# The returned rows of an expert stage: scaled on ScalarE, added on VectorE in groups of eight tiles

## What is computed

```python
x = x + 0.5 * L0_ffn(layernorm(x))      # stage 0, "f": experts
x = x + L0_attn(layernorm(x))           # stage 1, "s": scan
x = x + 0.5 * L0_ffn(layernorm(x))      # stage 2, "f": experts
x = x + 0.5 * L1_ffn(layernorm(x))      # stage 3, "m": soft mixture
x = x + L1_attn(layernorm(x))           # stage 4, "a": attention
x = x + 0.5 * L1_ffn(layernorm(x))      # stage 5, "m": soft mixture

# L0_ffn, for a token row x: one expert of eight, weighted by its probability
gate_probs = softmax(x @ gate_w.T)
e = argmax(gate_probs)
out = (relu(x @ w1[e] + b1[e]) @ w2[e] + b2[e]) * gate_probs[e]
```

## Time and profile before

| | us |
|---|---|
| median of 3 runs | 1003.56 |
| lowest and highest | 1002.2 and 1004.35 |
| the profiled execution | 1003.07 |
| span of its trace | 1001.3 |
| VectorE at L694, 64 instructions | 19.5 |
| VectorE idle until the returned rows land, twice | 14.2 |

### The profile page before, as it was taken

The page is one execution under the profiler, slowest core; times in us unless marked ns, Lnnn a source line. Parts: engine busy times, 40 slices in busy tenths (PEclk is TensorE's granted clock), DMA queues, the critical chain, the costliest instruction groups (busy, mean ns, idle before and its releaser), DMA issues.

```text
span 1001.3 us, 18706 instructions
## 1 busy us (share of the span) xinstructions
PE 777.1 (78%) x5564; PEld 512.1 (51%) x5564; DVE 658.6 (66%) x2367; ACT 507.3 (51%) x1371; POOL 442.9 (44%) x563
## 2 busy tenths in 40 slices
PE   4788983798498960499666979988999899729977
PEld 3678872547288860377651323333333333327757
DVE  4565654775865548856387776877777886566634
ACT  5333331606133323866411466767767677687650
POOL 1047773400277762411156577486585633261100
PEclk9999997895599995699895678999989999959999
DMA  6731113002011113000021342242231200000002
GB/s 154 230 92 49 50 47 99 1 1 84 13 46 52 50 37 82 0 1 1 1 45 32 59 58 37 31 63 34 38 54 31 48 4 3 1 1 1 1 1 84
DMA packets 53426, 42.95 MB, mean 43 GB/s; under 512 B 9861, under 2 KB 48722, under 8 KB 53328
## 3 DMA queue, kind: packets, MB, share of 16 engines
q1 hardware_dynamic: 46784, 31.74, 15.4%
q0 software_dynamic: 4992, 9.32, 3.4%
q10 hardware_dynamic: 1552, 0.70, 0.3%
HBM read 18.27 MB, written 11.40 MB: 30 GB/s over the span
## 4 chain that ended last, share of the span: by engine, by line
PE 42%; DVE 18%; POOL 12%; issue 12%; ACT 9%; DMA 5%; ACTq 1%; DVEq 1%; POOLq 0%; SPq 0%
PE psum L1498 5%; POOL arena L832 4%; DMA result_rows<-arena,scatter_row 3%; PE psum L1269 3%; PE psum L747 3%; DVE half_stats L444 3%; PE psum L1483 2%; DVE cst L1565 2%; PE psum L1232 2%; PE psum L1241 2%; PE psum L1438 2%; PE psum L787 2%; DVE x L694 2%; PE psum L1332 2%; PE psum L799 2%
## 5 line engine op out<-in xcount | busy, mean ns | idle before, releaser
L1565 DVE CUSTOM_DVE_ANT_0 cst<-psum,rot 128x512 bf16<-128x512 f32 (+3 forms) x512 | 219.1, 487 | 64.4 <-PE psum L1470 54.8
L1627 ACT ACTIVATE arena<-psum 128x512 f32<-128x512 f32 (+1 forms) x384 | 178.3, 530 | 51.5 <-PE psum L1483 46.0
L832 POOL DMA_INDIRECT arena<-xhat_rows,gather_row x78 | 76.6, 982 | 148.3 <-DVE gather_row L634 125.2
L1470 PE MATMUL psum<-arena 48*128 48x512 bf16 (+3 forms) x512 | 121.8, 330 | 14.5 <-DVE row_max L1565 10.6
L1483 PE MATMUL psum<-arena 51*128 51x512 bf16 (+3 forms) x512 | 114.9, 315 | 8.8 <-ACT arena L1627 7.1
L1722 POOL TENSOR_SCALAR_AFFINE_SELECT arena<-arena 128x384 f32<-128x384 f32 x128 | 63.6, 521 | 96.4 <-ACT arena L1627 96.4
L1498 PE MATMUL psum<-arena 128*32 128x512 f32 (+3 forms) x1024 | 98.3, 482 | 7.5 <-POOL arena L1725 7.5
L841 POOL DMA_INDIRECT result_rows<-arena,scatter_row x78 | 79.1, 1014 | 30.2 <-issue 22.2
L787 PE MATMUL psum<-arena 128*128 128x128 f32 x624 | 87.5, 286 | 4.2 <-DVE arena L649 4.2
L799 PE MATMUL psum<-arena 128*128 x624 | 89.5, 287 | 0.3
L715 ACT ACTIVATE arena<-psum,gate_b1T 128x128 f32<-128x128 f32 x156 | 48.7, 363 | 68.1 <-PE psum L787 68.1
(11 more groups left out here) (247 smaller groups left out, 1649.1 us busy)
## 6 DMA issues: line engine op xcount, KB each, us to landing
arena<-cut SPq DMA_DIRECT2D x192, 64.0 KB
xhat_rows<-xh SPq DMA_DIRECT2D x16, 256.0 KB, 2.3
arena<-result_rows SPq DMA_DIRECT2D x8, 512.0 KB, 6.0
x<-in_L_attn_x SPq DMA_DIRECT2D x4, 512.0 KB, 7.4
arena<-in_L_ffn_w SPq DMA_DIRECT2D x1, 2048.0 KB, 9.6
out<-x SPq DMA_DIRECT2D x4, 512.0 KB, 3.2
arena<-xhat_rows,gather_row POOLq DMA_INDIRECT x78, 2.5
result_rows<-arena,scatter_row POOLq DMA_INDIRECT x78, 2.3
```

The costliest lines, as they stand in the source:

```text
L832: pool.indirect_dma_start(xg[:, j % AHEAD, :], None, xhat_dram, bass.IndirectOffsetOnAxis(gather_row[:, j:j + 1], 0)).then_inc(gathered[j ...
L1470: mm = pe.matmul(to[:, col:col + (k + 1) * P], q_stack[b % STACKS][rows, h, k * P:k * P + P], k_stack[b % STACKS][rows, h, 0:(k + 1) * P], ...
L1565: last = nc.vector.tensor_tensor_reduce(masked_scores[:, number % 2, col:col + n_keys], frm[:, col:col + n_keys], mask[:, S - n_keys:], 1. ...
L1627: nc.scalar.activation(prob_e[g % 2][:, j, first:last], bank[MAX_BANKS + number % EXP_BANKS][:, 0:last - first], ACT.Exp, scale=DH ** -0.5 ...
```

## The change

The probability is multiplied in on ScalarE, tile by tile and in place, into `yback`. A new semaphore, `weighted`, counts the tiles. VectorE waits for the eight of a group and adds them to x with one operation of 128 x 1024, which counts `x_done` by eight. ScalarE takes the roots of groups 0, 1 and 2 of the next stage in between: behind the multiplications of groups 1, 2 and 3. Where the next stage's program asks for a root that has been taken, it goes on.

```diff
                 for g in range(GROUPS):
-                    dve.wait_ge(back[g], at["back"][g] + 16)
-                    for t in range(GT * g, GT * g + GT):
-                        nc.vector.scalar_tensor_tensor(x[:, t, :], yback[:, t, :], prob[:, t:t + 1], x[:, t, :],
-                                                       ALU.mult, ALU.add).then_inc(x_done[n + 1], 1)
+                    tiles = slice(GT * g, GT * g + GT)
+                    dve.wait_ge(s["weighted"], at["weighted"] + GT * g + GT)
+                    nc.vector.tensor_tensor(x[:, tiles, :], yback[:, tiles, :], x[:, tiles, :], ALU.add).then_inc(x_done[n + 1], GT)
                     stats_after(dve, n + 1, g)
...
+                def weighted(g):
+                    act.wait_ge(back[g], at["back"][g] + 16)
+                    for t in range(GT * g, GT * g + GT):
+                        nc.scalar.activation(yback[:, t, :], yback[:, t, :], ACT.Copy, scale=r_t[:, 2, t:t + 1]).then_inc(s["weighted"], 1)
+
+                weighted(0)
+                for g in range(1, GROUPS):
+                    weighted(g)
+                    stats_root(act, n + 1, g - 1)
```

More of the change, by code:

```diff
@@ L540, in build @@
         FFN_COUNTS = dict(v=0, normed=BY_SCALAR, normed_v=BY_VECTOR, turned=T, xT_ready=B, gated=B, log_ready=1, exp_ready=1,
-                          one_ready=1, ranked=1, hot_ready=T, tile_ready=1, inverted=1, row_hot=1, lanes_ready=1, gather_ready=1, rows_ready=1, expert_ready=1, g_turned=ROWS,
+                          one_ready=1, ranked=1, hot_ready=T, tile_ready=1, inverted=1, row_hot=1, lanes_ready=1, gather_ready=1, weighted=T, rows_ready=1, expert_ready=1, g_turned=ROWS,
                           xgT=ROWS, h_mm=ROWS, w1_ready=ROWS, hT_ready=ROWS, hT_ready_a=ROWS, y_mm=ROWS, y_ready=ROWS)
```

## The result

The changed kernel takes **1013.48 us** (median; 1011.84 to 1015.17) against 1004.13 of the kernel before on the same chip: a ratio of **1.0092**, 95% interval 1.0074 to 1.0111. In a later comparison it was 1.0101 (1.0078 to 1.0125). The forecast was 1007.4 us with a range from 1004.8 to 1009.4: the direction was right, and the time lies outside. The profiled execution took 1013.44 us, 10.4 more than that of before.

What follows compares the result with a forecast made beforehand. The prediction took VectorE to bound the first end, and the second until its last variance, then ScalarE. Losses of 2.1 and 1.7 us, 3.8 in all, on the median of 1003.56 gave 1007.4 us, range 1004.8 to 1009.4.

Steps and rivals of the forecast that it cites:

- What VectorE saves: At both expert stages' ends: eight operations of 2.23 us become one of 1.2 us, saving 1.0 us a group.
- ScalarE's multiplication: At both ends: 0.30 us a tile, 2.5 us a group, with the first group's 2.5 us bare.
- Rival (4): At both ends: the multiplication costs 0.388 us a tile, 0.7 us more at each end, 1008.9; chance 0.13.
- Table load hidden: First end, ScalarE: the 1.28 us table load ends before the variance of 174.5, with 0.3 us to spare.
- First end, 2.1 us: First expert stage's end: normalising queues behind group 2's root, so group 3's root comes at 191.4, not 189.36: 2.1 us lost.
- the wait for TensorE: First end: ScalarE waits about 0.6 us for TensorE, whose clock is lower for its first 6.5 us of work.
- Second end, 1.7 us: Second expert stage's end: centring starts later, VectorE waits for GpSimd, group 3's variance comes at 404.75, not 403.06: 1.7 us lost.
- alternation: Second end: VectorE's shifts and last addition take turns with GpSimd's products, each held up by the other; addition at 402.0.
- Rivals (1) and (2): Second end: (1) VectorE keeps its turn, 1005.8 in all, chance 0.22; (2) no collision with GpSimd, 1004.9, chance 0.10.
- What follows is unchanged: Behind the first end: later stages run as before, so the loss stays at 2.1 us and nothing is added.
- the forecast's sum: Whole kernel: losses of 2.1 us at the first end and 1.7 at the second make 3.8 us.
- VectorE's last variance at the first end: First end: VectorE has group 3's variance at 186.9, long before ScalarE takes its root at 191.4.

Runs made afterwards that it cites:

- g_after: The changed kernel with 24 and 23 unused one-element VectorE operations ahead of the two ends' waits: 1006.58 us, 1.0038.
- a_again: The changed kernel, unchanged, run again for a second profile: 1.0101 against the kernel before.
- d_12: The kernel before with 12 unused statistics on VectorE, 4.02 us of delay, ahead of the second end's first multiply and add: 1.0057.
- e_early: The changed kernel, but ScalarE weights all four groups one behind the other, with no roots taken in between: 1006.01 us, 1.0016.
- e_half: The changed kernel with all four groups weighted first, no roots in between, and VectorE adding four tiles at a time: 1002.94 us, 0.9993.
- g_half: e_half with 18 unused one-element VectorE operations ahead of each end's wait: 1001.02 us, 0.9976.
- The variant: The changed kernel with all groups weighted first and four tiles per addition: 0.9993; with 18 unused VectorE operations ahead of each end, 0.9976.
- f_before: The kernel before with 12 unused one-element VectorE operations ahead of the second end's wait: 1004.53 us, 1.0018.
- f_128: The kernel before with 64 unused one-element VectorE operations ahead of each end's wait: 1004.51 us, 1.0018.
- f_after: The changed kernel with 28 unused one-element VectorE operations ahead of each end's wait: 1008.01 us, 1.0042.
- f_half: e_half with 24 unused one-element VectorE operations ahead of each end's wait: 1002.62 us, 0.9988.
- w_before: The kernel before with 16 unread TensorE products in its idle stretch ahead of the attention: 1.0009.

## Why the prediction was wrong, point by point

- **What VectorE saves** (1.2 us for eight tiles, 1.0 us a group): right, 1.23 us.
- **ScalarE's multiplication** (0.30 us a tile, 2.5 us bare): right, 0.29, and 171.33 - 168.79 = 2.54. Rival (4), at 0.388, is out. The estimate of 0.294 us worked out from the Trainium skill, ScalarE: Activation LUTs, "What ACT_TABLE_LOAD costs", agrees with the 0.29.
- **Table load hidden**: right, with 0.45 us to spare.
- **First end, 2.1 us**: 2.6, by the same steps. The term that was short is the wait for TensorE: the second copies waited 0.95 us, and TensorE's first 16 products took 3.79 us at the lower clock, where the forecast had the full one after 6.5 us of work; it came 7.8 us after TensorE had started. In g_after the end lost 2.9 us, in a_again, where the full clock came after 6, 1.8.
- **Second end, 1.7 us**: right, 1.7 in after and in g_after, with the forecast's sequence: centring at 396.39, 15.3 behind the landing (15.2 was forecast), a gap of 2.27 us on VectorE ended by GpSimd, and alternation. The variance of group 3 is there 26.7 us behind the landing (26.7 forecast, 25.0 in the earlier trace rows). Rivals (1) and (2) are out. The Trainium skill's rule in SBUF — State Buffer, "Who interferes with whom" (VectorE operations with two SBUF inputs and GpSimd operations that read SBUF exclude each other for a whole one), agrees with the trace's 3.42 us for two shifts, which take 1.28 where GpSimd is not in the way.
- **"What follows is unchanged"**: this is the step that failed. It was said of the stages behind the first end and taken for the second too, since the code there is the same. The chip's work isn't: 48 instructions fewer on VectorE move the reads of its code, and with them two bursts of DMAs go from 16.9 and 19.2 us to 22.4 and 21.8, and TensorE waits. That is 5.8 us in the profile, a term that the sum had at nothing. With the reads put back (g_after), the change as written measures 1.0038, **3.8 us, which is the forecast's sum**. That it agrees so closely is luck: the interval is 1.9 to 5.6, and the profiled execution, at 1008.86, was above its median by 2.3; it is 5.7 us late at the attention's first product and loses 0.1 behind it. Of these 5.7 us the two ends are 4.6, and 0.9 was there when the first rows landed. So the change loses about what was forecast, and more than as much again by where it leaves the rest of VectorE's code.
- The range was worked out from the ends alone and so could not hold this. The pure delays show the same: 4.0 us of it cost 5.7 (d_12), whose first burst is slow too.
- One figure of the working is off: VectorE's last variance at the first end would by its own periods come at 186.6, not 186.9. Nothing rests on it.

## What to carry to other kernels

Moving work from a busy engine to one that idles gained nothing here, since the idle one also has the next step on the path: order its queue by what is waited for next (e_early), and cut the consumer's operation so that it can start on half of it (e_half, g_half). When a loss turns up in code that was not touched, compare the times of the same instructions one by one until the first that is late, look at what it waits for, and then at every queue in that stretch, those of instructions too. Before an edit that adds or removes instructions is judged at the level of 0.5%, measure it once more with the count made up by unused ones in an idle stretch, and take the count from the trace, waits with the rest (48 here, not 56). That moved the changed kernel from 1.0092 to 1.0038. The variant went from 0.9993 (0.9979 to 1.0006) to 0.9976 (0.9960 to 0.9991): it beats both kernels, though its two intervals overlap.

## What the runs showed of the hardware

- Stacking DMAs (SBUF to SBUF, packets of 1 KB), issued at equal intervals, were carried at 66 or at 94 and more packets a us, and what differs in the traces is whether an 8-KB read of VectorE's instructions fell at their start. Of four runs made with a forecast of the first burst, f_before and f_128 turned out so, and f_after and f_half did not, as the read missed the start; with other counts g_after and g_half did.
- 128 unused operations move VectorE's reads by one whole read (f_128: -0.11 us where before has -0.12): 64 bytes an instruction. The waits that stand as instructions of their own count too.
- The granted clock at the attention's start can be raised earlier (w_before: 34.1 us at the lower level instead of 47.8) without gain (1.0009, 0.9997 to 1.0021) where TensorE waits for others.
- One scaling of 128x128 on ScalarE by a column of the token's factors, SBUF to SBUF, is spaced 0.29 us; an addition of 128x1024 on VectorE takes 1.23 us, of 128x512 0.69 (after, e_half).
